# A decoder layer on one core: the barrier between two stages removed, the middle layer of the expert tiles turned, and the parts of 6 and 2 groups made 5 and 3

## The chip, the core and the metric

The kernel runs on one core of one Trainium2 chip. The metric is the device time of one execution in microseconds (us). The core has a matrix engine (TensorE, "PE" in the profile, its weight loads "PEld"), a vector engine (VectorE, "DVE"), a scalar engine (ScalarE, "ACT"), GpSimd ("POOL") and SyncE ("SP"), which here only starts transfers. Each engine runs its own list of instructions in order; semaphores alone tie them together. PSUM has eight banks into which TensorE writes and from which VectorE and ScalarE take results out.

## The reference

Input x is 4 sequences of 1024 rows of 256 numbers, float32, with a context of 64 rows for each sequence. One decoder layer is computed:

```
h  = layernorm(x)
q, k, v = silu(causal conv of 4 taps (h @ W.T))        # 4 heads of 64
beta    = sigmoid(h @ Wb.T)
q, k = q/|q|, k/|k|                                    # rnorm
for every chunk of 32 rows:                            # delta rule
    A    = strict_lower((k*beta) @ k.T)
    Tinv = inverse(eye + A)                            # triangular solve
    u, w = Tinv @ (v*beta), Tinv @ (k*beta)
    u    = u - w @ S ; o = q @ S + lower(q @ k.T) @ u ; S = S + k.T @ u
short, long = causal convs of v with 3 and 31 taps
o = mix of short, long, delta, v by a small gating network; RMS norm
x = x + o @ Wo.T
x = x + cross_attention(layernorm(x), context)         # 16 heads
f = layernorm(x)
s = sigmoid(f @ Wr.T + bias); top 2 of 8 experts; each chosen expert's
out = (silu(f @ G.T) * (f @ U.T)) @ Dn.T,  weighted by a mean weight per expert
x = x + sum of the two experts' outputs + a shared expert of 256 hidden columns
```

The mean weight of an expert is taken over all rows that chose it, so the weights are known only when every group has been routed.

## The kernel before

The 4096 rows are eight groups of 512 (NG = 8), each four tiles of 128 rows (T = 4). All engines' programs stand in one function, `decoder`, and the order of work on each engine is written out by hand; there is no planner.

**First stage, 0 to 197 us.** For each group, the rows are normed (VectorE), turned by TensorE (`hidden_rows`), copied by ScalarE into `hsT`, projected in six banks (`project`, L424), copied by ScalarE, convolved on VectorE (`conv`: four taps of 128x512 each, L1444, the first tap is ScalarE's, L953), passed through silu and squared on ScalarE (L964); `square_sums` and `rnorm` make the norms of q and k. There is one `hsT`: the next group's rows are turned after the six projections of the present one. All results are stored to DRAM.

**Between the stages, 197 to 272.3 us.** For group 0 `front_values` turns keys and values back to rows (TensorE L490, ScalarE copies), `front_rows` multiplies them by their scales (GpSimd L1289), `front_gram` computes A and its transpose (TensorE L502, VectorE L1525), GpSimd copies the 32x32 blocks on the diagonal of A out (L1310), `front_units` transposes them (VectorE L1535), the triangular solve follows (`first_solve` on VectorE, L1546 and L1548, for group 0; `front_steps` on GpSimd, L1326 and L1328, for the groups after it), then `front_compact` (VectorE L1558) and four block copies (`front_blocks`, ScalarE L1021). Beside this TensorE computes the long filter of 31 taps for all eight groups (16 calls of `long_filter`), ScalarE evacuates it and VectorE transposes it (`long_turned`, L1512) into `kq[1]`, from which it is stored. A semaphore `phase`, to which GpSimd, SyncE and VectorE each add one, holds TensorE, ScalarE and GpSimd before the first body; after it VectorE clears `Tf`, `MT` and `S`.

**Bodies 0 to 7, 272.3 to 1135 us.** `body(i)` does the delta rule, gates and output projection of group i. Woven into it are the cross attention and the router of group i - 1, its shared expert (`late_in`, `late_out`, `late`), and the front part (values, grams, units, solve, blocks) of group i + 1. For routed experts, `positions` and `ranks` count each row's place among the rows of its expert (TensorE and VectorE), `slots` makes addresses of it, and GpSimd's `scatter` (L1265, eight indirect DMAs a group) writes each row to its slot in DRAM.

**Last stage, 1135 to 1394.5 us.** Routed rows are handled in tiles of 128 slots that belong to one expert. The groups form two parts: `FIRST = (0, 6, NG)`, part 0 has groups 0 to 5 with 55 tiles, part 1 groups 6 and 7 with 23. When the last slots of a part are known, `tiles(h)` (VectorE, L1734 first) makes words that hold each tile's expert and place, `pads(h)` (GpSimd, L1275, eight indirect DMAs) fills the slots that no row took, and SyncE loads the words (`tile_rows`) and then the tiles' rows (`load_tile`). `pads(0)` and `tiles(0)` stand in body 7. The cross attention, router and shared expert of group 7 are woven into the first tile steps. In `tile_step(n)` TensorE turns the rows of tile n + 2 (L844), multiplies those of n + 1 (`gate_and_up`), turns the hidden rows of tile n (`hidden_turned`) and multiplies those of n - 1 (`down`):

```
for c in range(CK):                                          # L851
    mm(gu bank, stationary xTs[n % 2, c],  moving gate|up weights, 256 columns)
tr(hT bank, hm[n % 2])                                       # L859, then a DVE copy
mm(y bank, stationary hT[n % 2], moving down weights, 256 columns)   # L864
```

The weights are read in place, at an address that depends on the tile's expert. ScalarE copies the turned rows (L930) and computes silu of the gate (L1148), VectorE forms the product (L1956), copies hT (L1962) and takes the result out (L1969 to L1973), and GpSimd writes it to its rows by an indirect DMA (`place`, L1377). Once all results of a part are placed, SyncE fetches two rows for each row (`fetch`, L2278) and VectorE adds them up with their weights (`combine`, L1999), 32 combinations in all. `PIECES` names the tile steps after which one combination stands (18 of them); the other 14 come after the last tile.

## Time and profile before

| | before |
|---|---|
| median of 3 runs | 1395.92 us (1392.02 to 1396.6) |
| profiled execution | 1396.35 us, span 1394.5 us |
| busy in the span: PE, PEld, DVE, ACT, POOL | 1137.9, 853.3, 890.9, 462.2, 565.2 us (82, 61, 64, 33, 41%) |
| DMA traffic | 119 MB, mean 85 GB/s |

By stretch, in microseconds:

| stretch | PE busy | DVE busy | clock granted to PE |
|---|---|---|---|
| 0 to 197, first stage | 153.56 | 147.67 | 0.90 |
| 197 to 272.3, between | 37.84 | 44.61 | 0.76 |
| 272.3 to 361, body 0 | 62.59 | 39.36 | 0.82 |
| 361 to 920, bodies 1 to 5 | 498.98 | 368.44 | 0.97 |
| 920 to 1032, body 6 | 99.94 | 72.50 | 0.95 |
| 1032 to 1135, body 7 | 92.53 | 72.46 | 0.98 |

The span is the time from the first to the last record of the profiled execution; its own time is a little longer. "Idle before" is the time in which an engine stood still ahead of an instruction, and the name behind the arrow is what ended it: an engine with tile and line, a DMA, "issue" (nothing that the profile shows), or "remote" (a queue that the profile cannot name). L12 is line 12 of the kernel. Busy shares are means over stages with different limits, so what counts is which engine works without pause in each stretch.

### The profile page before, as it was taken

To read this page: it belongs to the slowest core of one execution; us is meant where nothing else is said; L and a number is where in the kernel's file an instruction comes from. 1 tells how busy PE (TensorE), PEld (TensorE's weight loads), DVE (VectorE), ACT (ScalarE), POOL (GpSimd) and SP (SyncE) were. 2 spreads that over 40 slices of the span, in tenths; PEclk is the share of its full clock that TensorE was granted. 3 is DMA by queue.
4 is the path that set the end of the run, shared out by engine and by line. 5 is a ranking of instruction groups with operands and counts; after the bars stand their busy time and mean duration, and the time that the engine had idled before them with its cause. 6 is when DMAs were issued, how large, how long until landed. Compare 5 with 4: busy or idle time off the path is not lost. (4 is left out here: it accounts for less than half of the span.)

```text
span 1394.5 us, 22102 instructions
## 1 busy us (share of the span) xinstructions
PE 1137.9 (82%) x7496; PEld 853.3 (61%) x7496; DVE 890.9 (64%) x2378; ACT 462.2 (33%) x825; POOL 565.2 (41%) x1002
## 2 busy tenths in 40 slices
PE   5788879194898798899799799789889969877792
PEld 2455458173776676676586586576667747655571
DVE  5788756655566765766676675666587555654377
ACT  4575744112323412421322331331341324422230
POOL 4243443027126426434633823742641232315542
PEclk9799889597899999999999999999999989988896
DMA  6545331501001301210120120130110342313468
GB/s 161 160 124 159 109 119 64 188 33 60 16 1 39 111 16 39 76 46 23 48 95 1 54 107 1 54 111 1 38 54 24 144 159 72 96 43 118 126 210 315
DMA packets 77822, 119.00 MB, mean 85 GB/s; under 512 B 28304, under 2 KB 53392, under 8 KB 75536
## 3 DMA queue, kind: packets, MB, share of 16 engines
q1 hardware_dynamic: 70128, 96.78, 21.6%
q0 software_dynamic: 7584, 20.80, 4.1%
q8 instruction: 63, 1.03, 0.3%
q14 instruction: 47, 0.39, 0.1%
HBM read 66.47 MB, written 51.09 MB: 84 GB/s over the span
## 5 line engine op out<-in xcount | busy, mean ns | idle before, releaser
L930 ACT ACTIVATE arena<-bank 128x512 f32<-128x512 f32 (+1 forms) x318 | 167.0, 544 | 555.8 <-PE bank L565 136.0
L1444 DVE SCALAR_TENSOR_TENSOR arena<-arena,param 128x512 f32<-128x512 f32 x144 | 106.2, 749 | 37.2 <-ACT arena L953 33.5
L1377 POOL DMA_INDIRECT results<-arena x78 | 76.4, 979 | 129.0 <-DVE arena L1973 95.7
L424 PE MATMUL bank<-hsT,wt 128*128 128x512 f32 x192 | 100.9, 683 | 24.4 <-ACT hsT L930 24.4
L1326 POOL TENSOR_TENSOR arena<-arena 128x126 f32<-128x126 f32 (+22 forms) x217 | 91.3, 421 | 49.4 <-DVE arena L1535 33.5
L1310 POOL COPY arena<-arena 32x128 f32<-32x128 f32 x128 | 50.3, 393 | 108.9 <-DVE arena L1525 103.0
L658 PEld LDWEIGHTS bank<-arena 128*128 128x128 f32 x768 | 88.6, 192 | 5.9 <-issue 5.7
L1328 POOL TENSOR_TENSOR arena<-arena 128x126 f32<-128x126 f32 (+22 forms) x217 | 82.7, 381 | 17.0
L658 PE MATMUL bank<-arena 128*128 128x128 f32 x768 | 89.3, 275 | 0.0
L851 PE MATMUL bank<-arena 128*128 x312 | 88.5, 410 | 0.1
L1799 DVE TENSOR_TENSOR arena<-arena,bank 128x512 f32<-128x512 f32 x96 | 62.4, 683 | 38.9 <-PE bank L658 24.1
L407 PE MATMUL bank<-const,arena 128*128 128x128 f32 x256 | 38.5, 299 | 59.5 <-DVE arena L1418 36.7
L424 PEld LDWEIGHTS bank<-hsT,wt 128*128 128x128 f32 x192 | 41.1, 222 | 74.3 <-issue 49.1
L1265 POOL DMA_INDIRECT slots_x<-arena x64 | 63.1, 986 | 45.6 <-DVE arena L1727 28.0
L1289 POOL TENSOR_TENSOR arena<-arena,rb 128x256 f32<-128x256 f32 x32 | 19.6, 612 | 145.3 <-ACT arena L930 145.3
L1525 DVE SCALAR_TENSOR_TENSOR arena<-bank,sc,const 128x128 f32<-128x128 f32 x128 | 38.7, 343 | 61.3 <-PE bank L502 61.3
L618 PE MATMUL bank<-arena 128*128 128x256 f32 x128 | 44.2, 520 | 34.8 <-DVE arena L1666 34.8
L1956 DVE TENSOR_TENSOR arena<-bank,arena 128x128 f32<-128x128 f32 x78 | 22.5, 288 | 76.3 <-issue 24.8
L407 PEld LDWEIGHTS bank<-const,arena 128*128 128x128 f32 x256 | 31.6, 153 | 64.4 <-DVE arena L1418 26.6
L555 PE MATMUL bank<-arena 128*128 128x512 f32 x128 | 66.2, 599 | 2.0 <-ACT arena L930 1.8
L575 PE MATMUL bank<-Va,arena 128*128 128x128 f32 x512 | 64.3, 279 | 4.2 <-DVE arena L1633 2.9
L1621 DVE TENSOR_REDUCE top<-bank 128x8 f32<-128x512 f32 x64 | 43.8, 685 | 33.2 <-PE bank L556 31.1
(266 smaller groups left out, 2724.7 us busy)
## 6 DMA issues: line engine op xcount, KB each, us to landing
arena<-slots_x SPq DMA_DIRECT2D x78, 129.0 KB
xt<-x_in SPq DMA_DIRECT2D x16, 512.0 KB, 4.8
kq_T<-kq SPq DMA_DIRECT2D x8, 1024.0 KB, 3.8
kq<-kq_T SPq DMA_DIRECT2D x8, 1024.0 KB, 5.7
arena<-results SPq DMA_DIRECT2D x32, 256.0 KB
arena<-ffn_in SPq DMA_DIRECT2D x7, 768.0 KB, 4.2
vT<-v_T SPq DMA_DIRECT2D x8, 514.0 KB
hs_T<-hsT SPq DMA_DIRECT2D x8, 512.0 KB, 4.1
```

The costliest lines, as they stand in the source:

```text
L407: last = tr(o[:, t * P:(t + 1) * P], src[:, t, c * P:(c + 1) * P], ident)
L424: last = mm(o[:, :], wgt("kqv"[j // 2], c, D)[:, (j % 2) * P:(j % 2 + 1) * P], hsT[:, c, :], start=c == 0, stop=c == CK - 1)
L555: mm(ov, qx[:, c, t * P:(t + 1) * P], Kblk[:, c, :, :], start=True, stop=False)
L575: last = mm(o[:, at:at + P], PT[:, c, k * P:(k + 1) * P], window(Va[:, :, :], at), start=True, stop=True)
L658: last = mm(oo, NT[:, h, :], (Y if q == 1 else UW)[:, h, :], start=True, stop=True)
L851: last = mm(o[:, 0:2 * EI].rearrange("p (s n) -> p s n", s=2), xTs[:, n % 2, c, :], gate_up[:, bass.ds(tile_w[n], 1), 0:2, c, :].rearrange ...
L930: free(act.activation(out_, in_, func, **kw), name)
L1265: pool.indirect_dma_start(slots_x[PART[i]][:, :], bass.IndirectOffsetOnAxis(ap=slot_at[:, i * T + t, k:k + 1], axis=0), xn_f[:, t, :], Non ...
L1326: own.link(pool.tensor_tensor(tmp, rows32[:, m0:, k].unsqueeze(2).broadcast_to([P, nm, k]), units[:, 0:k, k].unsqueeze(1).broadcast_to([P, ...
L1328: ins = pool.tensor_tensor(rows32[:, m0:, 0:k], rows32[:, m0:, 0:k], tmp, ALU.subtract)
L1377: pool.indirect_dma_start(results[:, :], bass.IndirectOffsetOnAxis(ap=dest[:, n % YS:n % YS + 1], axis=0), ys[:, n % YS, :], None).then_in ...
L1444: ins = V.scalar_tensor_tensor(cv[:, k % 4, :], pre[:, j, d:d + GT], param[:, at + d:at + d + 1], cv[:, k % 4, :], ALU.mult, ALU.add)
```

## The change

- A second buffer `hsT_b[1]` takes the turned rows of odd groups. `hidden_rows(i + 1)` stands after the fifth projection on TensorE, after the second copy group on ScalarE and after `conv(i, 1)` on VectorE.
- The scales of group 0 are computed in the first stage (at i = 3), those of the others later (`later_scales`).
- The barrier `phase` is gone. The turned long filter goes to `xt` instead of `kq[1]`, and `load_kq(1)` is issued with `load_kq(0)`. TensorE starts with `front_gram(0, 0)`; `front_values(0, t)` stands between the calls of `long_filter(1, t)`. VectorE clears `MT` and `S` first and runs grams, units, solve, the first half of the long filter's transposes, `front_compact(0)`, scales, second half. GpSimd starts with `front_solve(0)`, then `front_cleared(0)`, `rnorm(NG - 1)`, `front_rows(0)`, clears `Tf` when eight of the 16 long-filter results are turned, and makes the tables of the tiles.
- In body 0, the grams of group 1 stand between `solve(0)`, `solve(1)` and `solve(2)` and the units after `solve(3)`; on GpSimd solve and steps of group 1 come before its `front_rows`. In the later bodies VectorE runs `late()` before `front_compact` instead of after it.
- `FIRST` is (0, 5, NG): part 0 has 47 tiles, part 1 has 31. `tiles(0)` and `pads(0)` so stand in body 6, ahead of `front_rows` and the solve of group 7, and GpSimd waits for the pads before that solve. `PIECES` names 20 steps.
- In the tile loop ScalarE copies the gate and up weights of the tile's expert to `gu_w` (`weights(n)`, 128x512), with the expert read from the words by ScalarE too. They are the stationary operand, in four products of two passes each, 128 columns; `hm` comes out turned. `hidden_turned` and its copy are gone; `down(n)` takes `hm`, in step n, into banks 3 and 7 in turn.
- In the last stage `rows2` stands before the first five steps, `positions(NG - 1)` between the two halves of `late_in`, `slots` before `late()`, and `tiles(1)` has tile steps in its pauses. GpSimd does the last `scatter` after six places instead of seven, and without results placed between its eight DMAs.

```
-FIRST = (0, 6, NG)
+FIRST = (0, 5, NG)
 LEN = tuple(FIRST[h + 1] - FIRST[h] for h in range(PARTS))
 PART = tuple(h for h in range(PARTS) for _ in range(LEN[h]))
 REGION = tuple(LEN[h] * T + 1 for h in range(PARTS))
 NTILE = tuple(LEN[h] * T * 2 + E - 1 for h in range(PARTS))
 TILE0 = (0, NTILE[0], NTILE[0] + NTILE[1])

-PIECES = tuple(s for s in range(TILE0[1] + 6, TILE0[2] + 1))
+PIECES = tuple(s for s in range(TILE0[1] + 6, TILE0[2] + 1))[:FIRST[1] * T]
...
-        longT = kq[1][:, :, :, :].rearrange("p a b t -> p (a b) t")
+        a_ = LATE + n_ + T * D + 2 * QB * QB
+        assert a_ + CK * GT <= ARENA
+        hsT_b = [hsT, arena[:, a_:a_ + CK * GT].rearrange("p (c t) -> p c t", c=CK)]
+        longT = xt[:, :, :, :].rearrange("p g t d -> p (g t d)").rearrange("p (k n) -> p k n", k=4)
...
+                    if j == 4 and i + 1 < NG:
+                        hidden_rows(i + 1)
...
                     context()
                     rows()
+                else:
+                    keys_loaded(1)
+                    front_gram(1, 0)
+                    front_gram(1, 1)
                 solve(1)
                 if x:
                     queries()
+                else:
+                    front_gram(1, 2)
+                    front_gram(1, 3)
                 solve(2)
...
+            keys_loaded(0)
+            front_gram(0, 0)
+            pe.wait_ge(taps_loaded, 16 * CK * QB)
+            pe.wait_ge(sem("v_spread"), 2 * NG)
             for t in range(T):
-                front_values(0, t)
-                if t == 0:
-                    pe.wait_ge(taps_loaded, 16 * CK * QB)
-                    pe.wait_ge(sem("v_spread"), 2 * NG)
+                if t:
+                    front_gram(0, t)
                 long_filter(0, t)
             for t in range(T):
-                front_gram(0, t)
                 long_filter(0, 4 + t)
-            for k in range(8):
-                long_filter(1, k)
-            pe.wait_ge(phase, N_PHASE)
+            for t in range(T):
+                long_filter(1, t)
+                front_values(0, t)
+            for t in range(T):
+                long_filter(1, 4 + t)
             pe.wait_ge(setup_main, N_MAIN_SETUP)
...
-                for c in range(CK):
-                    last = mm(o[:, 0:2 * EI].rearrange("p (s n) -> p s n", s=2), xTs[:, n % 2, c, :],
-                              gate_up[:, bass.ds(tile_w[n], 1), 0:2, c, :].rearrange("p e s n -> p (e s) n"),
-                              start=c == 0, stop=c == CK - 1)
+                pe.wait_ge(sem("tile_weights"), n + 1)
+                for s_ in range(2):
+                    for c in range(CK):
+                        last = mm(o[:, s_ * P:(s_ + 1) * P], gu_w[:, n % 2, s_, c, :], xTs[:, n % 2, c, :],
+                                  start=c == 0, stop=c == CK - 1)
                 full(last, f"gu.{n}")

-            def hidden_turned(n):
-                o = open_bank(pe, f"hT.{n}", 3)
+            def down(n):
+                o = open_bank(pe, f"y.{n}", (3, 7)[n % 2])
                 drained(pe, f"gu.{n}")
-                full(tr(o[:, 0:P], hm[:, n % 2, :], ident), f"hT.{n}")
-
-            def down(n):
-                o = open_bank(pe, f"y.{n}", 7)
-                drained(pe, f"hT.{n}")
-                full(mm(o[:, 0:D], hT[:, n % 2, :], flat[:, bass.ds(tile_w[n] * (3 * D) + 2 * D, D)],
+                full(mm(o[:, 0:D], hm[:, n % 2, :], flat[:, bass.ds(tile_w[n] * (3 * D) + 2 * D, D)],
...
                 if 0 <= n + 1 < TILE0[2]:
                     gate_and_up(n + 1)
                 if 0 <= n < TILE0[2]:
-                    hidden_turned(n)
-                if 0 <= n - 1:
-                    down(n - 1)
+                    down(n)
...
             routing()
-            steps(2)
-            late_in(NG - 1, (None, None))
+            steps(1)
+            late_in(NG - 1, (None, None), ("lg",))
+            positions(NG - 1)
+            late_in(NG - 1, (None, None), ("lu",))
             steps(2)
             late_out(NG - 1, (None, None))
-            positions(NG - 1)
-            steps(8)
+            steps(7)
...
+                    if j == 1 and i + 1 < NG:
+                        hidden_rows(i + 1)
...
+            def weights(n):
+                if n >= 2:
+                    filled(act, f"gu.{n - 2}")
+                src = routed[:, bass.ds(tile_w[n], 1), 0:2 * D].rearrange("p e n -> p (e n)")
+                done(act.activation(gu_w[:, n % 2, :, :, :].rearrange("p s c n -> p (s c n)"), src, ACT.Copy),
+                     "tile_weights")
...
                     rows_turned(n + 2)
+                    weights(n + 2)
...
                 if i == FIRST[1] + 1:
                     pads(0)
-                if ahead:
+                if i == 0:
+                    front_solve(1)
+                    front_steps(1)
+                    front_rows(1)
+                elif ahead:
                     front_rows(i + 1)
                     if i >= 2:
                         h = PART[i - 2]
                         pool.wait_ge(sem(f"scattered{h}"), 32 * T * (i - 1 - FIRST[h]))
+                    if i == FIRST[1] + 1:
+                        pool.wait_ge(sem("padded0"), 16 * E)
                     front_solve(i + 1)
...
-            front_rows(0)
             front_solve(0)
             pool.sem_inc(sem("first_rows_set"), 1)
             front_cleared(0)
-            pool.wait_ge(phase, N_PHASE)
+            rnorm(NG - 1)
+            front_rows(0)
+            pool.wait_ge(sem("long_ready"), NG)
+            pool.memset(Tf, 0.0).then_inc(setup_main, 1)
+            pool.wait_ge(sem("long_ready"), CK * NG)
+            tile_tables()
...
-            place(7)
-            scatter(NG - 1, place)
+            place(6)
+            scatter(NG - 1)
             pads(PARTS - 1, place)
...
+                if i == 3:
+                    dve.wait_ge(sem("rnorm_ready"), 1)
+                    dve.wait_ge(sem("tanh_ready"), 1)
+                    scales(slice(0, 1))
...
+                if not x:
+                    filled(dve, f"N{T - 1}.{i}")
+                    front_gram(1, 0)
+                    front_gram(1, 1)
                 solve(1)
                 if x:
                     queries()
+                else:
+                    front_gram(1, 2)
+                    front_gram(1, 3)
                 solve(2)
                 if x:
                     scores(0)
                 solve(3)
                 if x:
                     scores(1)
+                else:
+                    front_units(1)
...
+                if x:
+                    late()
                 if ahead:
                     front_compact(i + 1)
-                if x:
-                    late()
...
-            dve.wait_ge(sem("scales_ready"), 1)
+            drained(dve, f"proj5.{NG - 1}")
+            for ins in (V.memset(MT, 0.0), V.memset(S, 0.0)):
+                ins.then_inc(setup_main, 1)
             for t in range(T):
                 front_gram(0, t)
-            dve.wait_ge(sem("kq1_stored"), 16 * B)
-            long_turned(0)
             front_units(0)
             first_solve()
+            long_turned(0)
+            front_compact(0)
+            later_scales()
             long_turned(1)
+            dve.wait_ge(setup_main, N_MAIN_SETUP)
             dve.wait_ge(sem("long_ready"), CK * NG)
-            dve.sem_inc(phase, 1)
-            dve.wait_ge(phase, N_PHASE)
-            for ins in (V.memset(Tf, 0.0), V.memset(MT, 0.0), V.memset(S, 0.0)):
-                ins.then_inc(setup_main, 1)
-            dve.wait_ge(setup_main, N_MAIN_SETUP)
-            front_compact(0)
...
             slots(NG - 2)
+            rows2()
...
             row_stats()
-            steps(4)
+            steps(3)
             rows3()
+            steps(1)
             routing()
+            steps(1)
             ranks(NG - 1)
-            steps(2)
+            slots(NG - 1)
             late()
-            steps(2)
+            tiles(PARTS - 1, lambda: steps(1))
             late_added()
-            slots(NG - 1)
-            tiles(PARTS - 1)
-            steps(4)
+            steps(3)
             weight_sums()
...
             sp.wait_ge(sem("squares_ready"), 4 * (NG - 1))
             load_kq(0)
+            sp.wait_ge(sem("kq1_stored"), 16 * B)
+            sp.wait_ge(sem("squares_ready"), 4 * NG)
+            load_kq(1)
```

## Rows read from the trace of the kernel before

**Rows 1.** Lines view, VectorE, 40 to 178 us: count, then busy and mean, then idle before.

```profile
L1444 DVE SCALAR_TENSOR_TENSOR arena<-arena,param 128x512 f32<-128x512 f32 x111 | 81.8, 749 | 26.8 <-ACT arena L953 24.1
```

**Rows 2.** Timeline, VectorE: start, duration, operation, and in brackets idle time and releaser.

```profile
108.64 2.33 DVE L1444 SCALAR_TENSOR_TENSOR arena<-arena,param 128x512 f32<-128x512 f32 x3 [1.79 <-ACT arena L953]
...
215.45 0.61 DVE L1525 SCALAR_TENSOR_TENSOR arena<-bank,sc,const 128x128 f32<-128x128 f32 x2 [11.34 <-PE bank L502]
...
233.92 1.20 DVE L1535 STREAM_TRANSPOSE arena<-arena 128x1024 f32<-128x1024 f32 x1
...
254.85 0.18 DVE L1548 TENSOR_TENSOR arena<-arena 128x16 f32<-128x16 f32 x1
...
258.05 2.74 DVE L1512 STREAM_TRANSPOSE kq<-arena 128x512 f32<-128x512 f32 x4 [0.31 <-DMA long_T<-kq]
...
348.77 0.71 DVE L1558 STREAM_TRANSPOSE arena<-arena 128x512 f32<-128x512 f32 x1 [6.40 <-POOL arena L1328]
...
968.78 0.61 DVE L1525 SCALAR_TENSOR_TENSOR arena<-bank,sc,const 128x128 f32<-128x128 f32 x2 [3.55 <-PE bank L502]
...
1077.05 0.36 DVE L1734 TENSOR_TENSOR arena<-arena 128x192 f32<-128x192 f32 x1
```

**Rows 3.** Timeline, TensorE.

```profile
202.84 0.66 PE L490 MATMUL bank<-const,kq 128*128 128x128 f32 x2 [5.80 <-DMA vT<-v_T]
...
272.32 6.43 PE L643 MATMUL bank<-arena 128*128 128x128 f32 x32 [30.95 <-issue]
...
282.15 10.88 PE L658 MATMUL bank<-arena 128*128 128x128 f32 x96
...
1253.92 0.47 PE L859 MATMUL bank<-const,arena 128*128 128x128 f32 x1 [5.35 <-DVE arena L1962]
```

**Rows 4.** Timeline, GpSimd (POOL).

```profile
226.23 1.76 POOL L1310 COPY arena<-arena 32x128 f32<-32x128 f32 x4 [1.32 <-DVE arena L1525]
...
319.62 0.25 POOL L1326 TENSOR_TENSOR arena<-arena 128x31 f32<-128x31 f32 x1 [2.76 <-DVE arena L1535]
...
986.45 0.26 POOL L1326 TENSOR_TENSOR arena<-arena 128x31 f32<-128x31 f32 x1 [5.12 <-DVE arena L1535]
...
1017.54 3.23 POOL L1357 TENSOR_TENSOR orn<-oss,minus_half 128x8 f32<-128x8 f32 x2
...
1083.35 0.96 POOL L1275 DMA_INDIRECT slots_x<-rows_of_no_token,arena  x1 [31.14 <-DVEq L1761]
...
1092.20 0.96 POOL L1275 DMA_INDIRECT slots_x<-rows_of_no_token,arena  x1 [0.30 <-issue]
```

**Rows 5.** Timeline, ScalarE (ACT).

```profile
267.77 4.34 ACT L1021 ACTIVATE arena<-arena 32x512 f32<-32x512 f32 x4 [25.33 <-DVE arena L1558]
```

**Rows 6.** Chain that ended last, one tile step of the last stage.

```profile
1288.06 0.87 PE bank L851 x4
1288.92 0.11 PE bank L859
1289.04 0.43 PE bank L864 x2
1289.47 0.22 PE bank L844 x2
```

**Rows 7.** Busy time by stretch: length, PE, PEld, DVE, ACT, POOL, clock, DMA, GB/s.

```profile
1135.00:1319.40 184.40, 146.04 (x684) 108.81 (x685) 92.19 (x374) 56.91 (x135) 74.90 (x78) 0.88 0.29 88
1319.40:1394.50 75.10, 46.41 (x219) 34.39 (x219) 53.69 (x195) 15.47 (x47) 27.09 (x28) 0.84 0.78 257
```

**Rows 8.** Lines view, ScalarE, 1135 to 1395 us.

```profile
L930 ACT ACTIVATE arena<-bank 128x256 f32<-128x256 f32 (+1 forms) x92 | 37.1, 415 | 114.1 <-PE bank L844 72.4 <-remote 16.9 <-issue 9.2
...
L1148 ACT ACTIVATE arena<-bank 128x128 f32<-128x128 f32 x78 | 21.6, 277 | 52.0 <-PE bank L851 20.9 <-issue 17.3 <-remote 13.6
```

**Rows 9.** Lines view, ScalarE and GpSimd, 0 to 330 us.

```profile
L964 ACT ACTIVATE kq<-arena 128x512 f32<-128x512 f32 x32 | 19.8, 618 | 2.5 <-DVE arena L1444 2.5
...
L1289 POOL TENSOR_TENSOR arena<-arena,rb 128x256 f32<-128x256 f32 x8 | 4.9, 613 | 37.2 <-ACT arena L930 37.2
```

164 lines of the change are left out of this document (86 added, 78 removed).

## The prediction

> **What bounds the kernel now.** I read the busy shares by stretch first, then the idle time of single engines at the seams, then the chain of waits. TensorE is busy 82% of the span, so the middle of the kernel, eight bodies of one group each, is nearly TensorE's. The change aims at the edges, and there other things end last.
>
> The first stage (projections and convolutions, about 197 us) is VectorE's. At each of seven seams between groups VectorE waits for the first tap of the next group; these waits are the 24.1 us in the group's row, 3.4 us a seam. The shortest was 1.79 us: there the projection was ready and only ScalarE's copy and first tap lay between [rows 1, 2].
>
> Between the stages TensorE stands still for 30.95 us, until 272.32 [rows 3]. The chain through it is on VectorE: the first gram block at 215.45, the last of four copies on GpSimd done at 228.0, the transpose of the units only at 233.92 because it stands behind eight transposes of the long filter, the first triangular solve until 255.03, eight more transposes, a barrier, three memsets, then ScalarE's four block copies from 267.77 to 272.1 [rows 2 to 5].
>
> In the first body VectorE then waits 6.40 us for GpSimd's solve of the next group, which ran from 319.62 to 348.7, 29.1 us [rows 2, 4]. In the seventh (group 6) GpSimd's solve ends at 1017.5, within a few tenths of a microsecond of when it is wanted: these two are in balance, and a later start of the solve is paid in full [rows 4].
>
> The last stage runs 78 tiles. A step that nothing disturbs is dense TensorE work: 0.22 + 0.87 + 0.11 + 0.43 = 1.63 us [rows 6]. But from 1135.0 to 1319.4 TensorE is idle for 184.4 - 146.0 = 38.4 us [rows 7]. One piece of 5.35 us is a wait for VectorE, which computes slots and tile words while nothing else can go on [rows 3]. ScalarE in the same stage shows 16.9 and 13.6 us of waits in front of two groups of instructions that end with nothing the profile can name ("remote"); those stand where GpSimd issues indirect DMAs one behind the other [rows 8].
>
> **The change part by part.**
>
> *A second hsT buffer, and the transposes of the next group earlier.* TensorE can project group i+1 at once, so a seam should shrink to the 1.79 us that ScalarE's two operations cost. 24.1 - 7 x 1.79 = 11.6 us; the scales of group 0, three short operations now in this stage, take some of it back (below 1 us). I take -11. The bounds are 0 (VectorE waits for another thing) and -12.
>
> *The barrier and the order between the stages.* The values' transposes came first and waited 5.80 us for a DMA, until 202.84 [rows 3]. Now the gram blocks come first; their keys are loaded long before, their scales are computed in the first stage, so TensorE starts them as soon as the last sums are done, at 197.0, and VectorE's first block falls from 215.45 to about 198.5: 17 us. The transpose of the units no longer stands behind the long filter's: it starts when GpSimd's copies end, 233.9 - 228.0 = 5.9 us. From the end of the solve to the first matmul of the body it was 272.3 - 255.0 = 17.3 us; now it is eight transposes (2 x 2.74 = 5.5), a memset on GpSimd, for which I take 2 (between nothing and the 4.34 of the block copies), the block copies 4.34 [rows 2, 5] and some tenths for semaphores and for the wait on a stored buffer, together 13: 4 us. Sum: -27. TensorE's filter work, idle-free from 197 instead of 203, is done some 10 us before it is wanted, so it is no bound. GpSimd's reciprocal roots of group 7 (behind the solve's set-up now) lie under the 20 us of the solve. Bounds: -32 (memset hidden, blocks free at once) to -13 (half, if the body's start hangs on a wait I did not see).
>
> *Grams of group 1 between the solves of body 0.* They keep TensorE in order behind VectorE's evictions, four times about 1.8 us, which is wholly lost at worst (7 us) and costs nothing if it is only moved. The GpSimd solve starts some 15 us earlier relative to the body, so the wait of 6.40 us goes; the eight row products that now come behind it on GpSimd (8 x 0.61 = 4.9 us [rows 9]) fit in that slack. -6.4 + 2.4 (a third of the 7) = -4. Bounds -6.4 and +1.
>
> *5 and 3 groups.* The tile count stays 78. The words of part 0 are computed in body 6 instead of 7. VectorE's share of that is 1083.35 - 1077.05 = 6.3 us, of which 3.55 us fall into the wait in front of group 7's first gram block [rows 2, 4]. Worse is GpSimd: its eight pads (1083.35 to 1093.2, 9.8 us) stand ahead of group 7's row products. In the time of this trace: VectorE ready at 965.2, words at 971.5, pads to 981.3, eight products 4.9, the start rows as long as one product, 0.6, four times four copies 7.0, so 993.8. The units' transpose (1.20 us, ending before the solve at 986.45) began at 985.2. The units and with them the solve of 31 us, which is in balance, start 8.6 us later: +9. Body 7 loses tiles and pads; TensorE was almost never idle there, so I give back 2 only. Net +7, bounds +2 (products and copies find slack) and +11.
>
> Of the 32 combinations, 20 now lie in tile steps and 12 behind the last, instead of 18 and 14. But all 12 are of part 1 and are fetched only after the last result, where 8 were; their 256 KB each go through two buffers of four. In the last stretch (75.1 us, DMA share 0.78 [rows 7]) I set the longer fetch against a shorter VectorE step and take 0, between -6 and +5.
>
> *The middle layer turned.* Weights become the stationary operand, so the hidden rows come out turned; the transpose on TensorE (0.11 us) and its copy on VectorE go. In place of two matmuls of 256 columns stand four of 128, in eight passes; such passes ran 96 in 10.88 us with a weight load each, 0.113 apart [rows 3], so 0.90 instead of 0.87. The step is 1.63 - 0.11 + 0.03 = 1.55 us, 0.08 x 55 steps to 1319.4 = -4.
>
> The price is on ScalarE: a copy of 128x512 of the tile's weights in each step. The same size took 0.62 us from SBUF to SBUF [rows 9], the strided block copies 4.34 / 4 = 1.08 [rows 5]. With 0.42 and 0.28 for its other two operations [rows 8] ScalarE needs 1.32, at worst 1.78 us a step. It is nearest to the plain copy, so I take 1.32: below TensorE's 1.55, cost nothing, but with 0.2 us left. Queued behind the copy are the gate, then VectorE's product, then the last matmul of the tile, which TensorE reaches 1.5 us after the gate's input; that is slack enough for 0.62.
>
> *Positions, slots and the tile words forward.* They run under the shared experts' matmuls, so the 5.35 us go; the rows of the last group's attention are normed before five steps instead of after them. The last scatter starts some 15 us earlier and without results between. Part 1 starts at tile 47 instead of 55, so it is needed 8 steps (13 us) earlier as well, behind 11 loads of words on SyncE instead of 8: a wait of up to 3 us there. Of 38.4 us idle I leave the 16.9 us of ScalarE's unnamed waits and 5.5 for the rest: -16. Bounds 0 (they grow with ScalarE's work) and -34.
>
> Sum: -11 - 27 - 4 + 7 - 4 - 16 = -55. The profiled execution took 1396.35 us (span 1394.5, about 1.9 us around it); the median is 1395.92, 0.4 us less. 1396.35 - 55 = **1341 us**.
>
> **The rivals.**
> *The tail gives nothing.* The indirect DMAs are as many, ScalarE stands still beside them as before, and it now has twice the work to catch up. For it: 16.9 + 13.6 us in [rows 8]. Against it: part of the idle time has VectorE's name. -35 instead of -55: 1361 us.
> *The tail gives nearly all.* The standstills fall under the shared experts' matmuls: -38 instead of -20, 1323 us.
> *The start of the bodies hangs on something else*, a memset or load now late: half the 27, so 1355 us. Against it: every input has 10 us in hand.
> *Weight loads exposed*, four more in each step: 78 x 4 x 0.113 = 35 us more, 1376 us. Against it: loads and matmuls went on together at 0.113 us a pair [rows 3].
> [...]
> *Slower than before: ScalarE bounds the tile loop.* If copy, dynamic address and waits bring its turn above 1.63 + 55/78 = 2.3 us a step, the whole gain is gone; at 3 us (all three operations one behind the other with TensorE's 0.9 and VectorE's product, nothing overlapping) the loop is 78 x 1.4 = 109 us longer less what TensorE was idle anyway, near 1410 us. Against it: the worst row gives 1.78.
> *The change does not do its work in the first stage*: seams stay at 3.4 us, 1352 us. It lies in the range.
>
> **How the numbers follow.** My forecast 0.47 (own range 1331 to 1352), tail nothing 0.19, tail all 0.14, start held or seams unchanged 0.14, weight loads 0.02, ScalarE the bound 0.04. Leaving out 2 in 10 gives 1320 to 1366. A measurement here tells about 0.3% (4 us). All cases but the ScalarE one are faster by far more: faster 0.94, same 0.02, slower 0.04.
>
> **What would show it.** VectorE's seams near 1.8 us; first body matmul 38 us earlier, at about 234, and TensorE idle some 10 us before it; the units of group 7 waiting for GpSimd, the body of group 6 about 7 us longer; no wait of TensorE for tile words after the shared experts; steps 1.55 us apart with ScalarE's turn at about 1.3. Wrong would be: steps at 1.8 us or more; ScalarE standing still longer in the scatters; a body 0 longer than before; TensorE waiting for tile 47.

## The result, and the profile after

The changed kernel takes 1334.72 us (median of 4 runs, 1334.11 to 1337.66) against 1396.26 us, a ratio of 0.957 with a 95% interval of 0.9546 to 0.9593. The forecast was 1341 us within 1320 to 1366. The profiled execution has a span of 1332.3 us against 1394.5, so 62.2 us are to be found in it. The marks are the first matmul of each body and the last matmul of `positions(6)` behind body 7:

| stretch | before | after | difference | predicted |
|---|---|---|---|---|
| first stage, to the end of the sums | 197.0 | 183.6 | -13.4 | -11 |
| from there to the first body | 75.3 | 58.9 | -16.4 | -27 |
| body 0 | 88.75 | 87.12 | -1.6 | -4 |
| bodies 1 to 5 | 559.24 | 551.34 | -7.9 | 0 |
| body 6 | 111.68 | 116.22 | +4.5 | +9 |
| body 7 | 100.5 | 99.2 | -1.3 | -2 |
| last stage | 262.0 | 235.9 | -26.1 | -20 |

The sum is right to 6 us and the terms are not: one gave 11 us less than was said, and one that was not in the working gave 8.

The first two rows have to be read together. Their common mark, the end of TensorE's last sums, moves from one execution of the same kernel to the next: it is at 183.6 here and at 186.95 in run 11, where the two stretches differ from the kernel before by -10.1 and -19.7. Both executions reach the first body at 242.5 to 242.6, 29.8 us earlier than before.

The seams of the first stage, in the lines view of VectorE of the changed kernel from 30 to 178 us (count, then busy and mean, then idle before):

```profile
L1490 DVE SCALAR_TENSOR_TENSOR arena<-arena,param 128x512 f32<-128x512 f32 x133 | 97.8, 749 | 15.7 <-ACT arena L963 12.3
```

12.3 us instead of 24.1 [rows 1]. Each of the seven seams is now 1.72 to 1.79 us. VectorE's transposes behind the last convolution, before and after:

```profile
193.40 2.01 DVE L1455 STREAM_TRANSPOSE arena<-vT 128x512 f32<-128x512 f32 x2 [0.70 <-ACT vT L964]
...
183.41 1.99 DVE L1501 STREAM_TRANSPOSE arena<-vT 128x512 f32<-128x512 f32 x2 [0.70 <-ACT vT L974]
```

By this mark the stage is 10.0 us shorter. The other 3.4 us of the -13.4 are TensorE's: its 32 last sums took 3.84 us at a granted clock of 1.00 and, before, 5.47 us at 0.70, each time behind a wait of 3.1 to 3.2 us. In run 11 the same kernel took 5.44 us at 0.69 for them, so this is no work of the change.

Between the stages, the timelines of TensorE, SyncE, VectorE, GpSimd and ScalarE of the changed kernel (start, duration, operation, idle time before and its releaser):

```profile
179.76 3.84 PE L446 MATMUL bank<-const,arena 128*128 128x128 f32 x32 [3.23 <-ACT arena L980]
191.01 2.08 PE L506 MATMUL bank<-kq 64*128 64x256 f32 x8 [7.42 <-issue]
...
183.40 0.57 SPq L2211 DMA_DIRECT2D v_T<-vT  x1
184.06 1.43 SPq L2173 DMA_DIRECT2D kq<-kq_T  x2
...
193.09 0.61 DVE L1580 SCALAR_TENSOR_TENSOR arena<-bank,sc,const 128x128 f32<-128x128 f32 x2 [6.10 <-PE bank L506]
...
206.69 1.25 DVE L1590 STREAM_TRANSPOSE arena<-arena 128x1024 f32<-128x1024 f32 x1 [1.59 <-POOL arena L1348]
...
236.29 1.81 POOL L1409 MEMSET arena<- 128x2048 f32 x1 [11.73 <-DVE xt L1567]
...
238.13 4.32 ACT L1035 ACTIVATE arena<-arena 32x512 f32<-32x512 f32 x4 [7.76 <-POOL arena L1409]
...
242.54 5.72 PE L649 MATMUL bank<-arena 128*128 128x128 f32 x32 [13.26 <-issue]
```

TensorE ends the last sums at 183.60 and stands still for 7.42 us before the first gram block. SyncE issues the load of group 0's keys only at 184.06, behind the store of the last group's values; it lands at 190.8, and the block's first matmul starts at 191.01. In run 11, TensorE:

```profile
181.51 5.44 PE L446 MATMUL bank<-const,arena 128*128 128x128 f32 x32 [3.11 <-ACT arena L980]
191.37 1.77 PE L506 MATMUL bank<-kq 64*128 64x256 f32 x8 [4.42 <-issue]
```

Here the load lands at 191.2. The wait is 4.4 or 7.4 us long according to when the sums end; the landing of the load sets its end. From the sums' end in this profile to VectorE's first block it is 9.5 us (18.4 before), from there to the units 13.6 (18.5 before) [rows 2]. The chain through the memset (1.81) and the block copies (4.32) is the one predicted.

In the bodies, the row of the page for the shared expert's last matmuls, before:

```profile
L618 PE MATMUL bank<-arena 128*128 128x256 f32 x128 | 44.2, 520 | 34.8 <-DVE arena L1666 34.8
```

and after:

```profile
L624 PE MATMUL bank<-arena 128*128 128x256 f32 x128 | 43.7, 517 | 26.2 <-DVE arena L1721 26.2
```

L1666 and L1721 are the same line, the product that `late()` computes on VectorE. TensorE waits 8.6 us less for it.

In body 6 GpSimd, in the changed kernel (timeline):

```profile
931.60 0.96 POOL L1310 DMA_INDIRECT slots_x<-rows_of_no_token,arena  x1 [32.07 <-DVEq L1818]
...
941.42 0.63 POOL L1324 TENSOR_TENSOR arena<-arena,rb 128x256 f32<-128x256 f32 x1
...
946.63 7.20 POOL L1348 COPY arena<-arena 32x128 f32<-32x128 f32 x16
...
955.26 0.25 POOL L1364 TENSOR_TENSOR arena<-arena 128x31 f32<-128x31 f32 x1 [1.43 <-DVE arena L1590]
```

Eight pads, eight products, 16 copies, then the solve. It starts 955.26 - 881.00 = 74.3 us into the body; before it was 986.45 - 920.31 = 66.1 [rows 4]. These 8.1 us are the 8.6 of the prediction.

In the last stage, undisturbed tile steps on TensorE:

```profile
1257.69 0.38 PE L859 MATMUL bank<-const,arena 128*128 128x128 f32 x2
1257.90 1.06 PE L868 MATMUL bank<-arena 128*128 128x128 f32 x8
1258.80 0.60 PE L875 MATMUL bank<-arena 128*128 x2
1259.23 0.38 PE L859 MATMUL bank<-const,arena 128*128 128x128 f32 x2
```

1259.23 - 1257.69 = 1.54 us a step (1.63 before [rows 6]), with eight passes of 128 columns and a weight load for each. In the page's row for these passes (count, busy and mean, idle before):

```profile
L868 PE MATMUL bank<-arena 128*128 128x128 f32 x624 | 88.9, 289 | 0.7 <-ACT arena L1179 0.3
```

TensorE stands still for 0.7 us in front of all 624, and the eight passes take 0.90 us (1257.90 to 1258.80), where four of 256 columns, with half as many loads, took 0.87 [rows 6]: nothing of the loads is exposed, or 0.03 us a step at most. ScalarE and VectorE in steps with a combination:

```profile
1285.91 0.38 ACT L940 ACTIVATE arena<-bank 128x256 f32<-128x256 f32 x1 [0.54 <-PE bank L859]
1286.19 0.62 ACT L1179 ACTIVATE arena<-arena 128x512 f32 x1
1286.81 0.28 ACT L1163 ACTIVATE arena<-bank 128x128 f32<-128x128 f32 x1
...
1285.81 0.28 DVE L2023 TENSOR_TENSOR arena<-bank,arena 128x128 f32<-128x128 f32 x1
1286.01 0.21 DVE L2030 SCALAR_TENSOR_TENSOR arena<-arena 128x1 f32<-128x1 f32 x1
1286.14 0.42 DVE L2032 COPY arena<-bank 128x256 f32<-128x256 f32 x1
1286.47 0.15 DVE L2034 TENSOR_TENSOR arena<-arena 128x1 int32<-128x1 f32 x1
1286.54 0.99 DVE L2058 SCALAR_TENSOR_TENSOR kq<-arena,kq 128x256 f32<-128x256 f32 x2
1287.45 0.29 DVE L2023 TENSOR_TENSOR arena<-bank,arena 128x128 f32<-128x128 f32 x1
```

The copy of the weights takes 0.62 us, ScalarE's turn is 1.28. VectorE has no idle time between these rows: with a combination it sets the pace, 1287.45 - 1285.81 = 1.64 us a step. With the hidden rows' copy (0.28, of which 0.2 are seen in the pace) it would be 1.84, the step with the old layer (run 2 shows it).

### The profile page after: what moved, and what is told of

Read it like the earlier page. It is cut to its first block and busy times, and to the rows that moved or that the text cites. A ratio compares the mean times of both kernels' runs of the same rounds, so it can differ in the third digit from the quotient of the medians.

```text
span 1332.3 us, 22522 instructions
## 1 busy us (share of the span) xinstructions
PE 1122.7 (84%) x7730; PEld 861.5 (65%) x7730; DVE 876.8 (66%) x2302; ACT 502.3 (38%) x904; POOL 561.4 (42%) x1003
## 5 line engine op out<-in xcount | busy, mean ns | idle before, releaser
L940 ACT ACTIVATE arena<-bank 128x512 f32<-128x512 f32 (+1 forms) x326 | 171.5, 546 | 518.6 <-PE bank L569 135.2
L1348 POOL COPY arena<-arena 32x128 f32<-32x128 f32 x128 | 50.3, 393 | 116.4 <-DVE arena L1580 110.2
L664 PEld LDWEIGHTS bank<-arena 128*128 128x128 f32 x768 | 91.8, 198 | 6.6 <-issue 6.4
L664 PE MATMUL bank<-arena 128*128 128x128 f32 x768 | 92.8, 281 | 0.0
L408 PE MATMUL bank<-const,arena 128*128 128x128 f32 x256 | 41.7, 316 | 57.3 <-DVE arena L1464 42.7
L868 PE MATMUL bank<-arena 128*128 128x128 f32 x624 | 88.9, 289 | 0.7 <-ACT arena L1179 0.3
L868 PEld LDWEIGHTS bank<-arena 128*128 128x128 f32 x624 | 82.0, 205 | 2.1 <-issue 1.8
L1859 DVE TENSOR_TENSOR arena<-arena,bank 128x512 f32<-128x512 f32 x96 | 62.3, 683 | 28.8 <-PE bank L664 14.6
L559 PE MATMUL bank<-arena 128*128 128x512 f32 x128 | 66.1, 598 | 1.8 <-ACT arena L940 1.8
L579 PEld LDWEIGHTS bank<-Va,arena 128*128 128x128 f32 x512 | 61.6, 196 | 9.2 <-DVE arena L1688 8.5
L624 PE MATMUL bank<-arena 128*128 128x256 f32 x128 | 43.7, 517 | 26.2 <-DVE arena L1721 26.2
L1676 DVE TENSOR_REDUCE top<-bank 128x8 f32<-128x512 f32 x64 | 43.8, 684 | 31.9 <-PE bank L560 31.8
L1112 ACT ACTIVATE wt<-bank 64x128 f32<-64x128 f32 x64 | 17.3, 271 | 119.9 <-PE bank L746 104.8
```

Of the source, the lines that this page charges most:

```text
L408: last = tr(o[:, t * P:(t + 1) * P], src[:, t, c * P:(c + 1) * P], ident)
L559: mm(ov, qx[:, c, t * P:(t + 1) * P], Kblk[:, c, :, :], start=True, stop=False)
L579: last = mm(o[:, at:at + P], PT[:, c, k * P:(k + 1) * P], window(Va[:, :, :], at), start=True, stop=True)
L664: last = mm(oo, NT[:, h, :], (Y if q == 1 else UW)[:, h, :], start=True, stop=True)
L868: last = mm(o[:, s_ * P:(s_ + 1) * P], gu_w[:, n % 2, s_, c, :], xTs[:, n % 2, c, :], start=c == 0, stop=c == CK - 1)
L940: free(act.activation(out_, in_, func, **kw), name)
```

## The experiments

Twelve runs were made, each beside the kernel before. Runs 1 to 4 ran on one chip, 5 to 8 on a second, 9 and 10 on a third, 11 and 12 on a fourth. Runs 1 to 4 and the last two ran where the kernel before takes 1396 to 1398 us (one place, in what follows), the six between where it takes 1374 to 1377 us (the other place); so ratios are compared within a place, and for single stages the traces are. In the other place the changed kernel itself did not run. The changed kernel once more (run 11) gave 0.9563 (0.9544 to 0.9581); with 0.957 from the result the yardstick for runs 1 to 4 is 0.9566, and a difference of two ratios is known to some 3 us.

### 1. Parts of 6 and 2

```diff
-FIRST = (0, 5, NG)
+FIRST = (0, 6, NG)
```

> The changed kernel with parts of 6 and 2 groups again, nothing else undone. The traces show body 6 at 116.2 us after against 111.7 before. If the pads and tile words ahead of group 7's solve are what makes it longer, body 6 falls back by 4 to 5 us, body 7 takes 1 to 2 of it (it has the words and pads again), and the last stage is 1 to 2 us longer, since 14 combinations instead of 12 stand behind the last tile at 0.92 us each: 1331 to 1334 us. Rival: the parts of 5 and 3 are needed for the last stage (part 1's rows come late, results wait): then body 6 falls all the same, but the last stage grows by more than 5 us and the time is 1336 us or more.

Measured: 0.9559 (0.9542 to 0.9575), no difference from the changed kernel. In its trace body 6 takes 111.3 us (116.2), body 7 1.4 us more, and the last stage 243.8 us. The last stage of the changed kernel took 235.9 and 239.9 us in its two traces, so up to 4 us of the 8 are within what it varies by. In this run the parts of 5 and 3 pay in body 6 what they give behind it. The expected fall of body 6 came; the two totals that were expected (1331 to 1334, 1336 or more) are not told apart.

### 2. The middle layer as before

```diff
-                for s_ in range(2):
-                    for c in range(CK):
-                        last = mm(o[:, s_ * P:(s_ + 1) * P], gu_w[:, n % 2, s_, c, :], xTs[:, n % 2, c, :],
-                                  start=c == 0, stop=c == CK - 1)
+                for c in range(CK):
+                    last = mm(o[:, 0:2 * EI].rearrange("p (s n) -> p s n", s=2), xTs[:, n % 2, c, :],
+                              gate_up[:, bass.ds(tile_w[n], 1), 0:2, c, :].rearrange("p e s n -> p (e s) n"),
+                              start=c == 0, stop=c == CK - 1)
...
-                    down(n)
+                    hidden_turned(n)
+                if 0 <= n - 1:
+                    down(n - 1)
...
-                    weights(n + 2)
```

> The changed kernel with the middle layer of the tiles as before (no copy of weights on ScalarE, hidden rows turned on TensorE and copied on VectorE). If a step costs what the undisturbed ones showed, 1.63 against 1.55 us on TensorE for 58 steps (+4.6) and 1.84 against 1.64 us on VectorE for the 20 steps with a combination (+4), the time is 1334.7 + 8.6 = 1343 us. First rival: ScalarE's copy costs as much in its standstills as the layer saves, within 2 us of 1334.7. Second rival: the turned layer is what took 26 us out of the last stage, 1350 us or more.

Measured: 0.9637 (0.9619 to 0.9656), so 0.0071 x 1396 = 10 us slower than the changed kernel, by the two steps' arithmetic 8.6. Both rivals fall. VectorE in this kernel, the products of two tiles one after the other:

```profile
1299.79 0.28 DVE L2007 TENSOR_TENSOR arena<-bank,arena 128x128 f32<-128x128 f32 x1
...
1301.63 0.28 DVE L2007 TENSOR_TENSOR arena<-bank,arena 128x128 f32<-128x128 f32 x1
```

The step with a combination is back at 1.84 us. The layer is worth 10 us, give or take 3; 4 were predicted. Missing were the 20 steps with a combination, where VectorE sets the pace: with the layer turned they lose 0.2 us each, 4 us.

### 3. The keys of group 0 loaded earlier

```diff
+                if i == NG - 1:
+                    sp.wait_ge(sem("kq0_stored"), 16 * B)
+                    sp.wait_ge(sem("squares_ready"), 4 * (NG - 1))
+                    load_kq(0)
                 sp.wait_ge(sem("act_ready"), 6 * i + 4)
...
-            load_kq(0)
```

> The changed kernel with one line moved on SyncE: group 0's keys are loaded before the last group's keys and values are stored, instead of behind them. If the 7.42 us that TensorE stood still before the first gram block are the load's issue behind these stores (issued at 184.1, landed at about 190), the first gram block is evicted right behind VectorE's two memsets, at 187.2 instead of 193.1, every later step of the chain moves by 6 us, and the time is 1329 us. Rival: TensorE waited for something else, or the chain is held by the long filter a step later: first body matmul within 2 us of 242.5 and no change in the time.

Measured: 0.9516 (0.9499 to 0.9533), 7 us faster than the changed kernel, where 6 were expected. The timelines of SyncE, TensorE and VectorE of this kernel:

```profile
173.64 0.36 SPq L2173 DMA_DIRECT2D kq<-kq_T  x1
...
181.67 5.47 PE L446 MATMUL bank<-const,arena 128*128 128x128 f32 x32 [3.11 <-ACT arena L980]
187.59 1.14 PE L506 MATMUL bank<-kq 64*128 64x256 f32 x8 [0.45 <-ACT st L940]
...
188.73 0.61 DVE L1580 SCALAR_TENSOR_TENSOR arena<-bank,sc,const 128x128 f32<-128x128 f32 x2 [1.27 <-PE bank L506]
...
237.24 6.66 PE L649 MATMUL bank<-arena 128*128 128x128 f32 x32 [13.57 <-issue]
```

The 7.42 us are 0.45, VectorE's first block comes 4.4 us earlier (188.73 for 193.09), and the first body starts at 237.24 instead of 242.54. The gain is less than 7.42 because the sums end at 187.14 here, as late as in run 11. The wait was the place of one load in SyncE's queue.

### 4. The last stage's order as before

```diff
-            steps(1)
-            late_in(NG - 1, (None, None), ("lg",))
-            positions(NG - 1)
-            late_in(NG - 1, (None, None), ("lu",))
+            steps(2)
+            late_in(NG - 1, (None, None))
             steps(2)
             late_out(NG - 1, (None, None))
-            steps(7)
+            positions(NG - 1)
+            steps(8)
...
-            place(6)
-            scatter(NG - 1)
+            place(7)
+            scatter(NG - 1, place)
```

and ScalarE's and VectorE's lists accordingly (`rows2`, `slots` and `tiles(1)` back in their places).

> The changed kernel with the last stage's order as before (attention rows normed after five steps, positions, slots and tile words behind the shared expert, the last scatter with results between). My prediction gave this order and the turned layer together 20 us, 16 of it from idle time; the traces show 26. If the order is the larger part, the 5 us wait for tile words is back and the time is 1334.7 + 10 to 16 = 1345 to 1351 us. Rival: the standstills beside GpSimd's indirect DMAs only move, and the order is worth 4 us or less: 1339 us or less.

Measured: 0.973 (0.9712 to 0.9747), 0.0164 x 1396 = 23 us slower, more than either theory. A part of it is a wait that neither kernel has; TensorE's timeline:

```profile
1276.09 0.66 PE L859 MATMUL bank<-const,arena 128*128 128x128 f32 x2 [9.73 <-DMA arena<-slots_x]
```

This is the first tile of part 1. With parts of 5 and 3 it is due 8 steps earlier, and in the old order its words and rows come late. The longest wait of this kind is 2.75 us in the changed kernel and 2.02 in the kernel before.

### 5. One buffer for the turned rows

```diff
-                    if j == 4 and i + 1 < NG:
-                        hidden_rows(i + 1)
...
                 beta_logits(i)
+                if i + 1 < NG:
+                    hidden_rows(i + 1)
```

with the two other engines and the buffer's waits accordingly.

> The changed kernel with one buffer for the turned rows and the next group's transposes behind the six projections again, nothing else undone. The prediction gave the second buffer 11 us; the seams measured 1.72 to 1.79 us after and 12.3 us in all against 24.1. If that is the buffer's work, the seams are back at 3 to 4 us each and the time is 1334.7 + 12 = 1346 to 1348 us. Rival: the seams are short because of another part (the place of the transposes on VectorE, the group's scales), 1337 us or less.

Measured: 0.9595 (0.9569 to 0.9621). VectorE's lines view of this kernel, 40 to 190 us, and TensorE's timeline:

```profile
L1490 DVE SCALAR_TENSOR_TENSOR arena<-arena,param 128x512 f32<-128x512 f32 x124 | 91.5, 750 | 27.3 <-ACT arena L963 24.2
```

```profile
200.41 1.81 PE L506 MATMUL bank<-kq 64*128 64x256 f32 x8 [4.31 <-issue]
```

The changed kernel did not run in this place, so the time that was expected is not tested. The seams are back at 24.2 us: they are the buffer's. At the first body 9.5 us are left of the 12 (it starts at 251.58 against 242.09 in run 7, which has the buffer and ran beside it). They are lost already in the first stage: VectorE's transposes behind the last convolution start at 192.80 against 183.30, with 46.6 and 36.6 us of idle time in front of them in all. So 12 us of seams are 10 us of idle time; the other 2 it had waited in front of other operations. The wait for the keys has no part in it: it is 4.31 us here and 4.42 in run 7.

### 6. The last scatter paced

```diff
                             xn_f[:, t, :], None).then_inc(sem(f"scattered{PART[i]}"), 16)
+                        if paced:
+                            pool.wait_ge(sem(f"scattered{PART[i]}"),
+                                         16 * (2 * T * (i - FIRST[PART[i]]) + 2 * t + k + 1))
```

the pads likewise.

> The changed kernel in which GpSimd waits for each indirect DMA of the last scatter and the last pads to land before it starts the next (the other work is the same). ScalarE's waits without a name were 28.3 us after, most of them between 1196 and 1231 us, while GpSimd issues an indirect DMA every 1.27 us. If they come from that row of DMAs one behind the other (something of ScalarE's has to get past them), they fall to less than half, though the scatter and the pads take longer, and the time lies within 5 us of 1334.7. Rival: they have nothing to do with the spacing: 24 us or more stay, and the later slots cost TensorE 5 to 15 us at tile 47.

Measured: 0.9729 (0.9706 to 0.9751), the last stage takes 241.5 us, 25 to 28 more than in runs 5, 9 and 10, whose last stage is the changed one. The question can't be answered by it: in this place the waits without a name are absent from every kernel, paced or not. The cost is not the one that the rival named either: TensorE's waits for tile rows are 7.9 us, 5.8 to 7.8 in those three. What it does show is VectorE's row in the waits of 1096 to 1338 us (in all, times, longest):

```profile
DVE arena L2035 <- DMA results<-arena: 31.8, 9, 5.9
```

VectorE waits 31.8 us for buffers whose results GpSimd has not placed, a wait that is not among the longest in runs 5 and 9: held up in its scatter, GpSimd holds up the tiles.

### 7. ScalarE with more to copy

```diff
+                for more in (more_a, more_b):
+                    act.activation(more[:, n % 2, :], src[:, 0:96], ACT.Copy)
```

> The changed kernel with two more copies of 128x96 on ScalarE behind each copy of a tile's weights (results not used). ScalarE's turn was 0.38 + 0.62 + 0.28 = 1.28 us against TensorE's 1.55 and VectorE's 1.64 with a combination. If a copy of 96 columns costs about 0.25, the turn is about 1.78, ScalarE sets the pace of undisturbed steps, and 58 steps become 0.2 and 20 steps 0.15 us longer: +10 to +18 us, 1345 to 1353 us. Rival: the tile loop is held by waits in which ScalarE has time enough: 1339 us or less.

Measured: 0.9583 (0.9564 to 0.9602); the last stage takes 219.5 us, against 213.1, 213.3 and 217.0 in runs 5, 9 and 10, whose last stage is the changed one. ScalarE's timeline:

```profile
1265.60 0.38 ACT L942 ACTIVATE arena<-bank 128x256 f32<-128x256 f32 x1
1265.88 0.62 ACT L1181 ACTIVATE arena<-arena 128x512 f32 x1
1266.40 0.44 ACT L1184 ACTIVATE arena<-arena 128x96 f32 x2
1266.75 0.27 ACT L1165 ACTIVATE arena<-bank 128x128 f32<-128x128 f32 x1
1267.25 0.38 ACT L942 ACTIVATE arena<-bank 128x256 f32<-128x256 f32 x1 [0.24 <-PE bank L861]
```

The two copies cost 0.35 us, not 0.5 (1266.40 to 1266.75). The step shown is 1.65 us from one row of L942 to the next, and 0.24 of them are idle time: ScalarE is at work for 1.4 us, still below TensorE's 1.54. Where nothing disturbs, from 1239.95 to 1252.77, eight steps take 1.60 us each, where they took 1.54 or 1.55. 0.35 x 78 = 27 us of work cost 2.5 to 6.4 us, so most of the copies fell into idle time. The forecast of 10 to 18 us rested on 0.5 us for the two copies. Whether ScalarE sets the pace from 1.55 us on is not shown, since the copies came out too short to pass TensorE.

### 8. Order and parts as before

The edits of 1 and 4 together.

> The changed kernel with the last stage's order and the parts of 6 and 2 groups both as before (the middle layer stays turned). With the old order alone TensorE stood 9.73 us before tile 47, for rows of part 1 whose words came late. If that wait belongs to the pair of old order and parts of 5 and 3, it is gone here since part 1 begins at tile 55: last stage 250 to 254 us instead of 260.8, body 6 4.9 us shorter, 1345 to 1349 us. Rival: the old order costs its 22 us with either parts: 1354 us or more.

Measured: 0.9607 (0.9586 to 0.9628), in another place than 4, so the last stages can't be set against each other; 230.1 us against 213.1 to 217.0 beside it are 13 to 17 us for order and parts together. Body 6 takes 111.0 us, 5.4 less than beside it, where 4.9 were expected. TensorE's waits for tile rows are 10.6 us, the longest (6.35 us, now before the first tile of part 1 at 55) is there still. The wait therefore does not belong to the parts of 5 and 3 alone; why the kernel before has none at that tile stays open.

### 9. `late()` behind `front_compact`

```diff
-                if x:
-                    late()
                 if ahead:
                     front_compact(i + 1)
+                if x:
+                    late()
```

> The changed kernel with VectorE's late() behind front_compact in each body again, as before. Bodies 1 to 5 took 551.3 us after against 559.2 before, which the prediction did not see. If the order of these two (so the shared expert's sums are taken before the wait for the solve) is the cause, they are back near 557 us or more: 1340 us. Rival: the bodies differ from run to run by that much (body 3 took 109.3 to 112.7 us in kernels that do not differ there): within 2 us of 1334.7.

Measured: 0.9644 (0.9622 to 0.9665). Bodies 0 to 6 together take 765.3 us against 755.4 in run 7, 9.9 us more, of which body 6 has 2.6 (119.0 against 116.4) and bodies 1 to 5 have 7.2. The row of the page:

```profile
L624 PE MATMUL bank<-arena 128*128 128x256 f32 x128 | 44.7, 524 | 36.0 <-DVE arena L1721 36.0
```

The wait of TensorE for `late()` is back from 26.2 to 36.0 us. The swap of two calls is the 8 us that the prediction did not have. The rival is wrong: bodies 1 to 5 take 559.3 us in this trace and 559.2 in that of the kernel before, and 548.8 to 552.7 us in the twelve traces with `late()` first.

### 10. Grams first, in two pairs of banks

```diff
-        o = [open_bank(pe, f"gram{t}{r}.{i}", (3, 7)[r]) for r in range(2)]
+        o = [open_bank(pe, f"gram{t}{r}.{i}", ((3, 7), (5, 6))[t % 2 if i == 0 else 0][r]) for r in range(2)]
...
+            for t in range(T):
+                front_gram(0, t)
             for t in range(T):
-                if t:
-                    front_gram(0, t)
                 long_filter(0, t)
```

on top of run 3.

> The kernel with group 0's keys loaded early, and its four grams ahead of the long filter, in two pairs of PSUM banks in turn instead of one pair. With one pair, each gram's matmuls (1.13) wait for VectorE to empty the banks (2.0), 3.07 us a block. If VectorE alone sets the pace, the blocks come 2.05 us apart, the solve starts 3 us earlier, and so does the first body: 1330.7 - 3 = 1327.5 us. Rival: GpSimd's copies (1.76 a block), or the long filter, which now starts 3 us later, take it back: 1330 us or more.

Measured: 0.9461 (0.9439 to 0.9484). VectorE's and TensorE's timelines:

```profile
188.36 0.61 DVE L1579 SCALAR_TENSOR_TENSOR arena<-bank,sc,const 128x128 f32<-128x128 f32 x2 [1.26 <-PE bank L506]
...
190.06 0.60 DVE L1579 SCALAR_TENSOR_TENSOR arena<-bank,sc,const 128x128 f32<-128x128 f32 x2
...
197.21 1.25 DVE L1589 STREAM_TRANSPOSE arena<-arena 128x1024 f32<-128x1024 f32 x1 [1.98 <-POOL arena L1347]
...
233.09 5.25 PE L649 MATMUL bank<-arena 128*128 128x128 f32 x32 [9.01 <-issue]
```

The blocks come 1.70 us apart instead of 3.07, the units start 4.1 us and the first body 4.2 us earlier than in run 3; 3 us were expected. The time itself can't be set against run 3's, which ran in one place and this in the other. The expectation's reading of the 3.07 us was not right: in run 3 TensorE has no pause there, it computes a gram (1.13) and then a call of the long filter (1.95), as its timeline shows:

```profile
188.66 1.95 PE L474 MATMUL bank<-arena 32*32 32x128 f32 x64
190.67 1.13 PE L506 MATMUL bank<-kq 64*128 64x256 f32 x8
```

So the order alone takes the filter out from between the blocks; what the second pair of banks adds was not run by itself. The long filter, later by 3 us, is not in the way: TensorE still waits 9.01 us before the body.

### 11. The changed kernel again

No edit.

> The changed kernel itself once more, as the yardstick of the last six runs: those ran where the kernel before takes 1374 to 1377 us instead of 1396 to 1398, and their traces show none of ScalarE's waits without a name. If these waits belong to the place and not to the kernel, the last stage takes 213 us here as in the two kernels whose last stage is the changed one (213.1 and 213.3) instead of 235.9, the bodies are unchanged, and the span is 1310 us. Rival: the kernels that ran there lacked the waits because of their edits: last stage above 225 us.

Measured: 0.9563 (0.9544 to 0.9581), 1335.82 us, so this run was not in the other place and does not test the forecast. The last stage took 239.9 us, ScalarE's waits without a name 21.8 us instead of 28.3. The stretch to the first body is told with the result.

### 12. Grams first, with parts of 6 and 2

The edits of 1 and 10 together.

> The kernel with early keys and grams first, with parts of 6 and 2 groups. Body 6 gives 5 us back (116.0 to 111.0) as it did in the other kernel with these parts. If the last stage took 8 us more there because of the waits without a name, which are absent here, it takes 2 us more (two more combinations of 0.92 us behind the last tile) and the time is 3 us below grams_first, ratio 0.944. Rival: the parts of 5 and 3 are worth 5 us or more in the last stage wherever it runs, and the two are equal, 0.946 or more.

Measured: 0.9462 (0.944 to 0.9485), 1319.42 us, where the changed kernel takes 1335.82. The interval holds both expectations, 0.944 and 0.946, and both counted on the other place, where run 10 has the same ratio. Beside run 11, which ran in the same place, the first body starts 7.4 us earlier, body 6 takes 109.6 us instead of 116.0, and the last stage 236.5 us instead of 239.9. Here the parts of 6 and 2 keep what they give in body 6; in run 1 they lost it behind it. Body 6 is 4.9 to 6.4 us shorter with them in all three traces that have them (runs 1, 8 and 12); what they cost in the last stage lies within what that stage varies by. By the ratios this kernel is 1.1% below the changed kernel and 5.4% below the kernel before.

## Why the prediction was right

The total was right to 6 us, and in part by luck: by the table, the stretches that gave less than was said miss 14 us (between the stages, bodies 0 and 7), those that gave more 21 us (the first stage, bodies 1 to 6, the last stage), and the two nearly cancel. Point by point:

- **Second buffer, -11.** Right: -10.0 by VectorE's end of the stage, with seams of 1.72 to 1.79 us where 1.79 was said, and 9.5 in run 5, which shows that the buffer does it. The -13.4 of the table hold 3.4 us that are not the buffer's.
- **Between the stages, -27.** Wrong in one step: "their keys are loaded long before, so TensorE starts them as soon as the last sums are done". The keys' load stood on SyncE behind the last group's stores and was issued after the sums. Of the 17 us for the first block 8.9 came in this profile (12.3 in run 11), and a wait of 7.42 us (4.42) took their place; run 3 removed it by moving the load. The other two steps were 4.9 instead of 5.9, and some 2.6 instead of 4. I had looked at the engines only, not at the queue on which the moved step's load stands.
- **Body 0, -4.** Measured -1.6. The wait for the solve is gone, 6.4 us. But the grams between the solves cost 6.4 us and not a third of 7: VectorE's gates (L1859 before, L1928 after) start 63.2 us into the body, at 305.70, instead of 56.8, at 329.12, and TensorE's pauses in front of the four grams are 5.5 us. The gain that is left came behind them.
- **Bodies 1 to 5, nothing.** Wrong, and by omission: the swap of `late()` and `front_compact` in VectorE's list was not costed at all. TensorE's wait of 34.8 us for that product was in the page. With `late()` ahead, it no longer stands behind a wait for GpSimd's solve. Run 9 gives 9.9 us for it, body 6 included.
- **Body 6 and 7, +7.** The mechanism and its size were right: the solve starts 8.1 us later into the body (8.6 said), and with `late()` in its old place body 6 takes 119.0 us, 7.3 more than before. The same swap takes 2.6 of these back. Of the 2 us in body 7 came 1.3.
- **Middle layer, -4.** Step and copy were right to a hundredth (1.54 for 1.55, 0.62 for 0.62), ScalarE's turn was 1.28 for 1.32. Measured is 10 us (run 2), of which VectorE's steps with a combination, which fell from 1.84 to 1.64 as well, are 4 by arithmetic; that gain had been set against the fetches, which cost nothing visible (from the last place to the end 20.6 us after, 21.1 before).
- **Order of the last stage, -16.** In the changed kernel it is worth 23 us (run 4); a wait of 9.73 us for tile 47 appears without it, and one of 6.35 us for tile 55 with the old parts (run 8). Order and layer together would be 33 us, the last stage fell by 26, so some 7 us of these overlap or go to the parts; runs 1 and 8 leave the size of that open.
- **Rivals.** Exposed weight loads and ScalarE as the bound fall, by the steps of 1.54 us and by run 7. In the tile steps the loads of the gate and up passes, 128x128 each, lie under the matmuls: 82.0 us of loads beside 88.9 us of matmuls, with 0.7 us of idle time before all 624 of these. "The tail gives nothing" rested on ScalarE's waits without a name. They stayed (28.3 us after, 30.5 before). Where they are missing, the kernel before is some 21 us faster and the changed last stage 19 to 27 us shorter, so they cost both kernels about alike.

## What to carry to other kernels

When work is moved ahead, follow the transfer that feeds it through the queue that issues it: a load behind two stores kept TensorE waiting for 4.4 to 7.4 us, and another place in the queue made the kernel 7 us faster. Cost swaps of two neighbouring calls too: the one that put VectorE's product ahead of its wait for GpSimd was worth 8 to 10 us. Add up a forecast's misses by stretch before trusting its total: here 14 us one way and 21 the other hid in a miss of 6. And look at which engine sets the pace in each kind of step: an operation removed from VectorE is worth most in the steps where VectorE is the bound (the turned layer took 0.2 us off each of these and 0.09 off the others).

## What the runs showed of the hardware

ScalarE's and VectorE's waits that end with nothing the profile can name go with the chip and not with the kernel, as far as these runs tell. In the place where the kernel before takes 1396 to 1398 us they are in all eight traces (in the last stage ScalarE 28.3 and 21.8 us in two executions of the same kernel; over the whole span VectorE 25 to 49 us in the eight); where it takes 1374 to 1377 us none of the six traces has one, in any stage, and the changed last stage is 213 to 217 us long instead of 236 to 240, while bodies 1 to 5 take the same 549 to 553 us in both. Busy time by stretch, first the changed kernel, then run 9, whose last stage is the same (length, TensorE, its loads, VectorE, ScalarE, GpSimd, clock, DMA share, GB/s):

```profile
1096.40:1332.30 235.90, 179.44 (x1138) 150.18 (x1137) 132.52 (x502) 111.59 (x260) 102.10 (x106) 0.90 0.47 151
```

```profile
1107.30:1320.60 213.30, 171.08 (x1137) 144.77 (x1137) 131.37 (x502) 112.36 (x260) 102.40 (x106) 0.92 0.51 167
```

The work is the same. TensorE's busy time differs by 8 us at a granted clock of 0.90 against 0.92, the rest is idle time. What uses the queue that the profile can't name was not found.
